# Filler matmuls on TensorE behind the last unit of the slot iterations and in the last normalisation

## The chip, the cores and the metric

One core of one Trainium2 chip runs the whole kernel as one launch. The metric is the device time in microseconds; the profile shows one execution of the same program.

## The reference

The computation is two layers on 16 batches of 56 tokens with 128 features, beside a context of 16 x 1500 x 128. What matters here is the second half:

```python
x = x + cross_attention_0(layernorm(x), ctx)      # 16 heads
x = x + ffn_0(layernorm(x))                       # fake-quantised, 384 wide
x = x + slot_attention(layernorm(x), ctx)         # 3 iterations, below
x = x + experts(layernorm(x))                     # 8 experts, 512 wide, summed

def slot_attention(slots, P):
    k, v = project(rmsnorm(P))
    for _ in range(3):
        q = rmsnorm(slots) @ Wq.T
        attn = softmax(q @ k.T * scale, axis=-2)  # over the 56 slots
        attn = attn / (sum(attn, axis=-1) + 1e-6)
        updates = attn @ v
        slots = gru_cell(updates, slots)
    return slots
```

The layer norm in front of the experts is the last normalisation: mean, centring, variance, square root, reciprocal, product.

## The kernel before

Tokens lie along the free dimension: `xT`, `stream` and the like are [128 features, 896 tokens]. PSUM is one tensor `ps` of eight banks of 512 fp32 columns; the banks 4 to 7 have names in the slot iterations: UPD (4), TURN (5), GATES (6), QUERY (7).

Each engine has a program of its own, written out by hand; an instruction starts when the one ahead of it on its engine lets it and when the semaphores waited for have come. There is no scheduler behind it.

**Slot iterations.** 3 iterations x 16 batches are 48 units of four slots each. In a unit TensorE makes the scores of one batch (L1590, 36 matmuls), VectorE finds the maxima and sums, ScalarE the exponentials (L784), GpSimd weighs them (L583). Four units are a quad; there are `GROUPS_C` = 12 quads, 4 per iteration. Each quad is followed by a string of stages, which `iterations` places some slots after the quad's begin, beside the units of later quads:

- `update_sums(0)` and `update_sums(1)` (offsets 19 and 27): the attend matmuls of two units each, L1606, into UPD
- `update_rows` on VectorE (L1203 to L1209): division by the sums
- `turn_updates` (offset 35): two transposes, L1616; ScalarE copies them out (L793)
- `gate_sums` (offset 39): six products in fp32 of `stream` and the copied updates, two passes each, L1624 to L1627
- ScalarE's tanh (L800, L806) and VectorE's GRU steps (L1218 to L1229), which write the new slots into `stream`
- `slot_means` (offset 51) and what follows from it up to the next queries, in bank QUERY: only for the quads 0 to 7, since the last iteration has no next queries.

For the last quad (11) the later stages come after the last unit's scores, in this order on TensorE: gates of quad 10, attend matmuls of the second pair of quad 11, its transposes, its gates. There is nothing else to do then.

**Last normalisation.** VectorE adds `stream` to `xT` (L1271, `x3_done`). `layernorm(3)` on TensorE makes the means (L1303, two fp32 products of 448 columns), waits for ScalarE's squares of what VectorE centred (L845, L635), makes the variance (L1308), waits for square root (ScalarE L640) and reciprocal (VectorE L849), and spreads the result over the rows (L1314). VectorE multiplies (L855) and splits the result in two fp16 halves (L1277, L1279). In VectorE's own queue, the first expert's weights are split on the way: `weights_high(0)` (L1263) behind the centring, `weights_low(0)` (L1267) behind the reciprocal. `layernorm` of TensorE takes two hooks, `after_means` and `after_variance`, which the fourth normalisation leaves empty.

**Experts.** 64 units (8 experts x 4 blocks x 2 halves of the tokens), nine fp16 products of 448 columns each (L1646 to L1648), whose results go through ScalarE (L823, L828), VectorE (L1285) and GpSimd (L619).

The kernel has a filler of the same sort elsewhere, `keep_busy`, in the feed-forward stage and in the third normalisation, whose lines are L1551 (means), L1554 (variance), L1512 (eight fillers) and L1559 (spread):

```python
def keep_busy(n):
    for _ in range(n):
        nc.tensor.matmul(ps[:, 5, 0:512], ctx_hi[:, 0, 0:128], ctx_hi[:, 0, 0:512], start=True, stop=True)
```

Of the kernel before, what the change touches and what calls it, by code (L numbers as in the profile page):

```python
# [65 lines left out]
def wait(engine, semaphore, value):  # L66

    if isinstance(value, int) and value <= 0:
        return
    engine.wait_ge(semaphore, value)  # L70
# [21 lines left out]
def build(nc, dram, out):  # L92
    with ExitStack() as ctx:
        def sbuf(name, shape, dt=F32, stack=ctx):
            return stack.enter_context(nc.sbuf_tensor(name, shape, dt))
# [4 lines left out]
        ps = ctx.enter_context(nc.psum_tensor("ps", [128, 8, 512], F32))  # L100
# [100 lines left out]
        query_hi = sbuf("query_hi", [128, T], F16, stack=sc)  # L201
# [38 lines left out]
        GROUPS_C = UNITS_C // QUAD  # L240
# [68 lines left out]
        UPD, TURN, GATES, QUERY = 4, 5, 6, 7  # L309
# [27 lines left out]
        def quad(g):  # L337
            return bass.ts(g % PER_IT, QT)
# [9 lines left out]
        def rows_of(n):  # L348

            return n % BATCH if n % BATCH < RESIDENT else RESIDENT + streamed_load(n) % STREAMED  # L350

        def rows_landed(n):

            return 16 if n % BATCH < RESIDENT else 16 * (streamed_load(n) // STREAMED + 1)
# [267 lines left out]
        def _(act):  # L622
# [7 lines left out]
            def layernorm_sd(n, after_squares=None):  # L630
                _, centred, squared, _ = NORMS[n]
                wide = WIDE[n]
                for h in range(2):
                    act.wait_ge(ln_centred, 2 * n + h + 1)
                    nc.scalar.activation(squared[:, bass.ts(h, wide)], centred[:, bass.ts(h, wide)], ACT.Square).then_inc(ln_squared, 1)  # L635
                if after_squares:
                    after_squares()
                act.wait_ge(ln_var, n + 1)
                wait(act, ln_rstd, n)
                nc.scalar.activation(sd[:, 0:wide // 2], ps[:, 2, 0:wide // 2], ACT.Sqrt, bias=eps_ln[:]).then_inc(ln_sd, 1)  # L640
# [121 lines left out]

            load_table(ACT.Sqrt)
            _, centred, squared, _ = NORMS[2]
            for h in range(2):
                act.wait_ge(ln_centred, 4 + h + 1)
# [70 lines left out]
        def _(dve):  # L837
            def layernorm(n, after_squares=None, after_roots=None):

                src, centred, _, dst = NORMS[n]  # L840
                wide = WIDE[n]
                for h in range(2):
                    at = bass.ts(h, wide)
                    dve.wait_ge(ln_mean, 2 * n + h + 1)
                    nc.vector.tensor_tensor(centred[:, at], src[:, at], ps[:, h, 0:wide], ALU.subtract).then_inc(ln_centred, 1)  # L845
                if after_squares:
                    after_squares()
                dve.wait_ge(ln_sd, n + 1)
                nc.vector.reciprocal(rstd[:, 0:wide // 2], sd[:, 0:wide // 2]).then_inc(ln_rstd, 1)  # L849
                if after_roots:  # L850
                    after_roots()
                for h in range(2):
                    at = bass.ts(h, wide)
                    dve.wait_ge(ln_spread, 2 * n + h + 1)
                    nc.vector.tensor_tensor(dst[:, at], centred[:, at], ps[:, SPREAD[n][h], 0:wide], ALU.mult).then_inc(ln_out, 1)  # L855
# [442 lines left out]
        def _(pe):  # L1298
            def layernorm(n, after_means=None, after_variance=None):
                src, _, squared, _ = NORMS[n]  # L1300
                wide = WIDE[n]
                for i in range(2):
                    nc.tensor.matmul(ps[:, i, 0:wide], ones_mean[:], src[:, bass.ts(i, wide)], start=True, stop=True).then_inc(ln_mean, 1)  # L1303
                if after_means:
                    after_means()
                pe.wait_ge(ln_squared, 2 * (n + 1))
                for i in range(4):
                    last = nc.tensor.matmul(ps[32 * i:32 * i + 32, 2, 0:wide // 2], ones_mean[:, 0:32], squared[:, bass.ts(i, wide // 2)], start=True, stop=True)  # L1308
                last.then_inc(ln_var, 1)
                if after_variance:  # L1310
                    after_variance()
                pe.wait_ge(ln_rstd, n + 1)
                for i in range(4):
                    last = nc.tensor.matmul(ps[:, SPREAD[n][i // 2], bass.ts(i % 2, wide // 2)], spread[:, i, :], rstd[:, 0:wide // 2], start=True, stop=True)  # L1314
                    if i % 2:
                        last.then_inc(ln_spread, 1)
# [213 lines left out]
            for i in range(4 * F0):  # L1530
                if i == 9:
# [4 lines left out]
                                 start=True, stop=True).then_inc(f_ready, 1)  # L1536
# [12 lines left out]
            _, _, squared, _ = NORMS[2]  # L1549
# [18 lines left out]
            def late_spread():  # L1568

                pe.wait_ge(ln_rstd, 3)  # L1570
                for i in range(4):
                    last = nc.tensor.matmul(ps[:, LATE_SPREAD + i // 2, bass.ts(i % 2, GW)], spread[:, i, :], rstd[:], start=True, stop=True)
                    if i % 2:
                        last.then_inc(ln_spread, 1)

            def unit(n, k):
# [14 lines left out]
                if k == SLOTS - 1:  # L1591
                    last.then_inc(c_scores, 1)
                    if n == 1:
                        late_spread()

            def update_sums(pair):
                def sums(g):
                    m = 2 * g + pair
                    pe.wait_ge(c_attended, 2 * m + 2)
                    for n in (2 * m, 2 * m + 1):  # L1600
                        pe.wait_ge(rows_loaded[rows_of(n)], rows_landed(n))
                    wait(pe, u_rows_done, g)
                    for c in range(NCH):
                        for j in range(2):
                            n = 2 * m + j
                            last = nc.tensor.matmul(ps[64 * j:64 * j + TOK, UPD, (D + 1) * pair:(D + 1) * (pair + 1)], c_prob[n % PROBS][:, c, :],  # L1606
                                                    ctx_rows[:, rows_of(n), c, :],
                                                    start=(c == 0), stop=(c == NCH - 1), skip_group_check=True)
                    last.then_inc(u_ready, 1)
                return sums  # L1610

            def turn_updates(g):
                pe.wait_ge(u_rows_done, g + 1)
                wait(pe, tanh_done, g)
                for i in range(2):
                    last = nc.tensor.transpose(ps[:, TURN, bass.ts(i, D)], u_rows[:, i, :], ident32[:])  # L1616
                last.then_inc(u_turned, 1)

            def gate_sums(g):
                slots = stream[:, quad(g)]  # L1620
                pe.wait_ge(u_copied, g + 1)
                wait(pe, slots_done, g)
                for i in range(2):
                    nc.tensor.matmul(ps[:, TURN, bass.ts(i, QT)], whhT[:, bass.ts(i, D)], slots, start=True, stop=False)  # L1624
                    nc.tensor.matmul(ps[:, TURN, bass.ts(i, QT)], to_gates[:, bass.ts(i, D)], updT, start=False, stop=True)
                nc.tensor.matmul(ps[:, GATES, QT:2 * QT], whhT[:, 2 * D:3 * D], slots, start=True, stop=True)
                nc.tensor.matmul(ps[:, GATES, 0:QT], to_gates[:, 2 * D:3 * D], updT, start=True, stop=True).then_inc(gates_ready, 1)  # L1627

            def slot_means(g):
# [4 lines left out]

            iterations(unit, [
                (TENSOR_AT["means"], True, slot_means), (TENSOR_AT["turn"], False, turn_updates), (TENSOR_AT["gates"], False, gate_sums),
                (TENSOR_AT["sums"][0], False, update_sums(0)), (TENSOR_AT["sums"][1], False, update_sums(1))])


            pe.wait_ge(x3_done, 1)  # L1640
            layernorm(3)

            def product(bank, w, w_at, x_high, x_low, first, last):

# [92 lines left out]
```

## Time and profile before

| | |
|---|---|
| median of the runs | 814.04 us |
| lowest and highest of 3 | 813.88, 817.6 us |
| the profiled execution | 809.81 us |
| its span, first to last instruction | 808.0 us |
| mean granted TensorE clock | 0.925 |
| TensorE busy | 683.6 us, 85% |
| VectorE, ScalarE, GpSimd busy | 581.7, 533.2, 435.5 us |

Busy time is a share of the whole span; the stages differ. The granted clock is the share of 2.4 GHz that TensorE was given; it has two levels here, 1.0 and 0.5, and a figure between them is a mean over a stretch that has both. A matmul's record holds the time in which its result drains, so neighbouring records overlap.

### The profile page before, as it was taken

To read this page: it belongs to the slowest core of one execution; us is meant where nothing else is said; L and a number is where in the kernel's file an instruction comes from. 1 tells how busy PE (TensorE), PEld (TensorE's weight loads), DVE (VectorE), ACT (ScalarE), POOL (GpSimd) and SP (SyncE) were. 2 spreads that over 40 slices of the span, in tenths; PEclk is the share of its full clock that TensorE was granted. 3 is DMA by queue.
4 is the path that set the end of the run, shared out by engine and by line. 5 is a ranking of instruction groups with operands and counts; after the bars stand their busy time and mean duration, and the time that the engine had idled before them with its cause. 6 is when DMAs were issued, how large, how long until landed. Compare 5 with 4: busy or idle time off the path is not lost.

```text
span 808.0 us, 23757 instructions
## 1 busy us (share of the span) xinstructions
PE 683.6 (85%) x8878; PEld 492.1 (61%) x8878; DVE 581.7 (72%) x1073; ACT 533.2 (66%) x1158; POOL 435.5 (54%) x476
## 2 busy tenths in 40 slices
PE   5789599999999999997835678888788875899997
PEld 2267377777777777775522468887778863444443
DVE  5878387878878787887786667778777755665663
ACT  3266276777777776765462699899988962555554
POOL 1647847777777777742000044666666520566664
PEclk9799699999999999999876979999888995999999
DMA  5532634444444444330500504532540540112100
GB/s 192 138 109 74 178 97 136 133 132 132 128 134 129 131 126 133 92 88 14 188 0 3 234 2 160 196 123 93 218 166 2 181 136 26 53 41 79 39 2 24
DMA packets 26720, 86.15 MB, mean 107 GB/s; under 512 B 5829, under 2 KB 7493, under 8 KB 26645
## 3 DMA queue, kind: packets, MB, share of 16 engines
q1 hardware_dynamic: 26264, 84.73, 33.1%
q8 instruction: 46, 0.75, 0.4%
q10 hardware_dynamic: 384, 0.46, 0.2%
q14 instruction: 26, 0.21, 0.1%
HBM read 65.19 MB, written 0.46 MB: 81 GB/s over the span
## 4 chain that ended last, share of the span: by engine, by line
PE 45%; DVE 17%; POOL 14%; ACT 9%; issue 8%; SPq 4%; DMA 2%; POOLq 0%; DVEq 0%; ACTq 0%
POOL ctx_lo L619 9%; PE ps L1350 8%; PE ps L1367 7%; PE ps L1381 6%; ACT c_prob L784 4%; PE ps L1337 4%; PE ps L1606 3%; SPq L436 3%; PE ps L1590 3%; PE ps L1326 3%; DVE tile_max L870 2%; PE ps L1386 2%; DVE ps L1171 2%; ACT w0T L784 2%; DVE amax_part L1086 1%
## 5 line engine op out<-in xcount | busy, mean ns | idle before, releaser
L870 DVE TENSOR_REDUCE tile_max<-ps 128x1 f32<-128x500 f32 x336 | 215.0, 675 | 51.4 <-PE ps L1350 51.0
L645 ACT ACTIVATE probs<-ps 125x896 f32<-125x896 f32 x192 | 175.3, 916 | 95.9 <-PE ps L1367 95.0
L1350 PE MATMUL ps<-k_hi,qdiag 128*128 128x500 f16 x336 | 130.4, 390 | 6.9 <-DVE tile_max L870 2.8
L784 ACT ACTIVATE c_prob<-ps,c_bias,row_scale 125x56 f32<-125x56 f32 x384 | 116.0, 473 | 6.9 <-DVE c_bias L1174 6.9
L619 POOL TENSOR_TENSOR ctx_lo<-ctx_hi,ctx_lo 128x448 f16<-128x448 f32 x64 | 72.1, 1127 | 70.7 <-ACT ctx_lo L828 70.7
L1367 PE MATMUL ps<-qstack,kstack 98*125 98x224 f16 x768 | 107.1, 263 | 0.4
L583 POOL TENSOR_TENSOR c_prob<-c_prob,c_weight 125x672 f32<-125x672 f32 x32 | 42.0, 1311 | 115.6 <-DVE c_weight L1188 115.5
L1367 PEld LDWEIGHTS ps<-qstack,kstack 98*125 98x125 f16 x768 | 86.7, 137 | 21.1 <-ACT probs L645 2.8
L1590 PE MATMUL ps<-query_hi,ctx_hi 128*128 128x56 f16 x576 | 55.9, 195 | 34.1 <-ACT c_prob L784 24.7
L1381 PE MATMUL ps<-probs,v_aug 125*32 125x168 f32 x1536 | 75.4, 314 | 3.3 <-ACT probs L645 2.5
L1590 PEld LDWEIGHTS ps<-query_hi,ctx_hi 128*128 128x128 f16 x576 | 49.6, 101 | 40.5 <-ACT c_prob L784 23.8
L1646 PE MATMUL ps<-ctx_lo 128*128 128x448 f16 x192 | 67.8, 353 | 6.9 <-DVE ctx_hi L1285 3.2
L538 POOL TENSOR_TENSOR rows_in<-rows_in 125x768 f32<-125x768 f32 (+2 forms) x96 | 68.8, 717 | 7.5
L1285 DVE SCALAR_TENSOR_TENSOR ctx_hi<-ctx_hi,ps 128x448 f32<-128x448 f32 x64 | 38.8, 616 | 45.4 <-ACT ctx_hi L823 45.4
L823 ACT ACTIVATE ctx_hi<-ps 128x448 f32<-128x448 f32 x64 | 34.8, 543 | 51.7 <-PE ps L1648 51.5
L523 POOL TENSOR_TENSOR qstack<-q_rep,slot_mask 96x224 f16<-96x224 f32 (+1 forms) x64 | 33.7, 556 | 63.2 <-PE ps L1367 58.1
L1648 PE MATMUL ps<-ctx_lo 128*128 128x448 f16 x192 | 67.7, 352 | 0.0
L1647 PE MATMUL ps<-ctx_lo 128*128 128x448 f16 x192 | 67.7, 352 | 0.0
L1171 DVE TENSOR_REDUCE ps<-ps 125x12 f32<-125x672 f32 x48 | 41.3, 860 | 26.9 <-PE ps L1590 26.9
L1381 PEld LDWEIGHTS ps<-probs,v_aug 125*32 125x32 f32 x1536 | 40.4, 109 | 32.3 <-issue 24.4
L1590 PE MATMUL ps<-query_hi,ctx_lo 128*128 128x56 f16 x576 | 55.8, 194 | 0.0
L1590 PE MATMUL ps<-query_lo,ctx_hi 128*128 128x56 f16 x576 | 55.6, 194 | 0.0
(262 smaller groups left out, 1702.4 us busy)
## 6 DMA issues: line engine op xcount, KB each, us to landing
row_tiles<-in_ctx_rows_wide SPq DMA_DIRECT2D x40, 774.0 KB, 5.7
ctx<-in_ctxT SPq DMA_DIRECT2D x16, 750.0 KB, 5.4
rows_in<-in_ctx_rows SPq DMA_DIRECT2D x16, 750.0 KB
kstack<-k_hi SPq DMA_DIRECT2D x128, 93.8 KB, 2.8
kstack<-k_lo SPq DMA_DIRECT2D x64, 93.8 KB, 2.7
ctx_hi<-in_wg SPq DMA_DIRECT2D x8, 256.0 KB, 2.7
ctx_hi<-in_wu SPq DMA_DIRECT2D x8, 256.0 KB, 3.0
ctx_hi<-in_wd SPq DMA_DIRECT2D x8, 256.0 KB, 3.5
```

Source lines behind the costliest of these rows:

```text
L538: nc.gpsimd.tensor_tensor(a, a, z, ALU.add).then_inc(rows_step, 1)
L619: nc.gpsimd.tensor_tensor(hidden_lo[i], hidden[i], hidden_hi[i], ALU.subtract).then_inc(h_lo_done, 1)
L645: nc.scalar.activation(probs[c % RING_P][0:CH, :].rearrange("p (k w) -> p k w", k=2), score_tile(c)[0:CH], ACT.Exp, scale=float(HD) ** -0. ...
L784: last = nc.scalar.activation(c_prob[n % PROBS][:, c, :], ps[0:CH, 2 * (n % 2) + c // 6, bass.ts(c % 6, TOK)], ACT.Exp, bias=c_bias[n % 2] ...
L870: nc.vector.reduce_max(tile_max[:, u % MAXT, u // MAXT:u // MAXT + 1], ps[:, MAXB + (u + p) % 2, 0:KCOLS], AX.X).then_inc(max_done, 1)
L1350: nc.tensor.matmul(ps[:, MAXB + (u + p) % 2, 0:KCOLS], qdiag[p][:, bass.ts(t, 128)], k_hi[p][:, bass.ts(j, KCOLS)], start=True, stop=True) ...
L1367: last = nc.tensor.matmul(ps[0:CH, 2 * (c % 2) + g // 2, bass.ts(g % 2, GW)], kstack[p][0:STACK_ROWS, g, bass.ts(c, CH)], qstack[p][0:STAC ...
L1381: nc.tensor.matmul(ps[GR * g:GR * g + GR, OUTB, 0:three], v_aug[p][0:CH, of, g, HD:], probs[of % RING_P][0:CH, GW * g:GW * g + three], sta ...
L1590: last = nc.tensor.matmul(ps[:, 2 * (n % 2) + c // 6, bass.ts(c % 6, TOK)], l, r, start=(j == 0), stop=(j == 2))
L1646: nc.tensor.matmul(bank, w1_hi[w][:, at], x_high, start=first, stop=False)
L1647: nc.tensor.matmul(bank, w1_lo[w][:, at], x_high, start=False, stop=False)
L1648: return nc.tensor.matmul(bank, w1_hi[w][:, at], x_low, start=False, stop=last)
```

## The change

A function `keep_warm(g, n)` issues n matmuls of [128x128] by [128x512] in fp16 into bank QUERY, for the last quad alone. It is called with 4 ahead of the second pair's attend matmuls, 4 ahead of the transposes and 3 ahead of the gates, each time before the waits of that stage; then with 18 ahead of the wait for `x3_done`, 5 behind the means, 7 behind the variance, and 9 behind the spread: 50 in all.

```diff
+            def keep_warm(g, n):
+
+                if g == GROUPS_C - 1:
+                    for _ in range(n):
+                        nc.tensor.matmul(ps[:, QUERY, 0:512], query_hi[:, 0:128], query_hi[:, 0:512], start=True, stop=True)
+
             def update_sums(pair):
                 def sums(g):
+                    keep_warm(g, 4 * pair)
                     m = 2 * g + pair
                     pe.wait_ge(c_attended, 2 * m + 2)
...
             def turn_updates(g):
+                keep_warm(g, 4)
                 pe.wait_ge(u_rows_done, g + 1)
...
             def gate_sums(g):
                 slots = stream[:, quad(g)]
+                keep_warm(g, 3)
                 pe.wait_ge(u_copied, g + 1)
...
+            last_quad = GROUPS_C - 1
+            keep_warm(last_quad, 18)
             pe.wait_ge(x3_done, 1)
-            layernorm(3)
+            layernorm(3, after_means=lambda: keep_warm(last_quad, 5), after_variance=lambda: keep_warm(last_quad, 7))
+            keep_warm(last_quad, 9)
```

## Rows read from the trace of the kernel before

**Rows 1.** The page, part 2: granted clock in 40 equal slices, in tenths.

```profile
PEclk9799699999999999999876979999888995999999
```

**Rows 2.** Stretches: their length, busy time of each engine (instructions), clock, DMA.

```profile
core 0: us, PE busy (x) PEld busy (x) DVE busy (x) ACT busy (x) POOL busy (x), PEclk, DMA share, GB/s
437.30:460.00 22.70, 16.61 (x144) 9.64 (x145) 11.98 (x18) 11.88 (x28) 0.00 (x0) 1.00 0.53 210
656.70:659.40 2.70, 2.54 (x12) 2.19 (x12) 1.29 (x4) 0.95 (x5) 0.90 (x3) 1.00 0.54 204
663.10:665.40 2.30, 0.62 (x6) 0.20 (x2) 1.82 (x6) 0.34 (x1) 0.00 (x0) 1.00 0.00 0
...
665.90:669.30 3.40, 3.40 (x11) 2.98 (x9) 0.00 (x0) 0.00 (x0) 0.00 (x0) 0.51 0.00 0
669.40:672.80 3.40, 0.23 (x2) 0.00 (x0) 2.08 (x6) 2.17 (x4) 0.00 (x0) 0.99 0.00 0
672.90:686.30 13.40, 7.68 (x20) 3.87 (x20) 7.59 (x9) 3.54 (x7) 0.00 (x0) 0.50 0.08 26
686.50:690.00 3.50, 1.62 (x9) 0.89 (x10) 1.76 (x3) 0.27 (x1) 0.00 (x0) 1.00 0.29 107
...
692.00:796.00 104.00, 101.00 (x528) 50.82 (x527) 64.36 (x74) 59.70 (x118) 66.91 (x60) 1.00 0.12 39
```

**Rows 3.** The chain that ended last, in order of time: start, length, what.

```profile
669.03 0.61 PE ps L1627 x2
...
674.72 3.37 PE ps L1303 x4
...
682.52 3.37 PE ps L1314 x8
...
685.91 0.63 DVE stream L855
```

**Rows 4.** TensorE in order of time; in brackets its idle time before, and the releaser.

```profile
660.41 0.32 PE L1606 MATMUL ps<-row_tiles,merge_w 125*56 125x129 f32 x1 [1.08 <-POOL w0T L583]
...
664.20 0.44 PE L1616 MATMUL ps<-ident,u_rows 128*128 128x128 f32 x2 [0.92 <-DVE u_rows L1209]
665.44 0.62 PE L1624 MATMUL ps<-stream,whhT 128*128 128x224 f32 x2 [0.80 <-DVE stream L1229]
...
674.72 3.35 PE L1303 MATMUL ps<-xT,ones_mean 128*128 128x448 f32 x4 [5.09 <-DVE xT L1271]
679.40 0.97 PE L1308 MATMUL ps<-work,ones_mean 128*32 128x224 f32 x8 [1.32 <-ACT work L635]
682.52 3.35 PE L1314 MATMUL ps<-rstd,spread 128*128 128x224 f32 x8 [2.15 <-DVE rstd L849]
688.38 0.36 PE L1646 MATMUL ps<-ctx_lo 128*128 128x448 f16 x1 [2.50 <-DVE ctx_lo L1279]
```

**Rows 5.** The same view of TensorE around the third normalisation.

```profile
434.68 2.34 PE L1512 MATMUL ps<-ctx_hi 128*128 128x512 f16 x5
...
443.21 1.77 PE L1551 MATMUL ps<-xT,ones_mean 128*128 128x448 f32 x4 [0.78 <-DVE xT L1133]
446.30 0.59 PE L1554 MATMUL ps<-work,ones_mean 128*32 128x224 f32 x8 [1.32 <-ACT work L767]
446.82 1.90 PE L1512 MATMUL ps<-ctx_hi 128*128 128x512 f16 x8
449.04 1.78 PE L1559 MATMUL ps<-work,spread 128*128 128x224 f32 x8 [0.32 <-DVE work L1142]
```

**Rows 6.** VectorE and ScalarE in order of time, in both normalisations.

```profile
447.44 1.55 DVE L1142 RECIPROCAL work<-work 128x224 f32<-128x224 f32 x1 [1.79 <-ACT work L769]
...
450.32 1.17 DVE L1149 TENSOR_TENSOR work<-work,ps 128x448 f32<-128x448 f32 x2
...
664.67 0.34 ACT L793 COPY work<-ps 128x224 f32<-128x224 f32 x1 [3.14 <-PE ps L1616]
...
680.92 1.55 DVE L849 RECIPROCAL rstd<-sd 128x224 f32<-128x224 f32 x1 [1.31 <-ACT sd L640]
682.39 1.70 DVE L1267 SCALAR_TENSOR_TENSOR ctx_lo<-ctx_hi,ctx_lo 128x1536 f16<-128x1536 f32 x1
```

## The prediction

> **What bounds the kernel now.** I read the slices of the page first, for the granted clock. The row of clocks [rows 1] is at 8 or 9 tenths over most of the span, and its lowest digit, a 5, stands in the seventh-last place, which at 20.2 us a slice is 667 to 687 us. That is where most of the added matmuls go. So the second view is a table of stretches around that place [rows 2]. The reader is to see three things in its clock column: TensorE holds its upper level (1.00, 2.4 GHz) until about 665.9 us; from there to 669.3 us it works with no idle at 0.51, the lower level (1.2 GHz); and after an interval at 0.99, in which it did next to nothing, it is at 0.50 again from 672.9 to 686.3 us. From 686.5 us it is at 1.00 to the end.
>
> Third, the chain of waits, to see whether the slow stretches set the end. They do: the chain [rows 3] goes through the last gate products, which begin at 665.44 us [rows 4] and end at 669.64 us, the four mean matmuls (3.37 us) and the spread (3.37 us), with the variance (0.97 us, [rows 4]) and steps of VectorE and ScalarE between them. Nothing runs beside these: all the units are finished, and every engine waits for this one string. The gates belong to the last quad; they are released by VectorE's L1229, the new slots of the quad before, and need the copy of this quad's updates as well.
>
> Behind it lies the expert stage, 119.6 us from 688.38 us on. There TensorE is busy 101.00 of 104 us at full clock [rows 2], so that stage has a length of its own, and whatever is won ahead of it moves its start and the end of the kernel alike. Its weights wait on nothing here: the first two experts' loads are issued when the last scores are done.
>
> **What the change adds.** Nothing is removed or moved. It adds 50 matmuls of 128x512 in fp16 (4, 4, 3, 18, 5, 7, 9 in program order), each with its weight load, all into bank 7, which nobody reads or writes in this part: its users, the slot means and projected queries, exist only for the first eight quads, and the copy of query_hi that the fills read is written no more. No fill signals anything and none waits; but what is queued behind a fill on TensorE waits for it. No DMA, and no work for another engine, is added.
>
> The price of one fill at the upper level: the expert stage did 528 matmuls of 448 columns in 101.00 us, 0.191 us each, so 512 columns are an estimated 0.219 us [rows 2]. The old kernel has the same kind of filler: eight of them took 1.90 us, 0.24 us each with the last one's drain [rows 5]. At the lower level five took 2.34 us; I take 0.44 us each, twice the first figure.
>
> Now each group of fills against the idle time of TensorE that it stands in [rows 4]:
> 4 fills, 0.88 us, ahead of L1606 (the last 48 attend matmuls): idle 1.08 us.
> 4 fills, 0.88 us, ahead of the transposes L1616: idle 0.92 us. This is the tight one, but the copy L793 that hangs on the transposes is done at 665.01 us [rows 6], 0.43 us before the gates start, so a small overrun is still covered.
> 3 fills, 0.66 us, ahead of the gates L1624: idle 0.80 us.
> 18 fills, 3.94 us, ahead of the means L1303: idle 5.09 us. Queued behind them are the means, and for those wait VectorE's centring and everything after.
> 5 fills, 1.10 us, ahead of the variance L1308: idle 1.32 us.
> 7 fills, 1.53 us, ahead of the spread L1314: idle 2.15 us.
> 9 fills, 1.97 us, ahead of the first expert product L1646: idle 2.50 us, and more once the spread is fast.
> All are covered at the upper level, so I cost them at nothing. If that cover is gone, that is, at the lower level, they overrun by 0.7, 0.8, 0.5, 2.8, 0.9, 0.9 and 1.5 us; 6.1 us for the last four, all on the chain.
>
> Could the fills slow VectorE or ScalarE through PSUM or SBUF? The reciprocal L1142 that ran beside eight fillers took 1.55 us, and L849, the same shape with TensorE idle, took 1.55 us [rows 6]. So zero, and the other bound is the rounding of these two rows.
>
> **What the clock gives back.** If the fills keep the clock up, four pieces shrink; each has a twin at the upper level in this same trace.
> Gates: 665.44 to 669.64 us is 4.20 us; the same twelve matmuls of the quad before were busy 2.54 us [rows 2 to 4]. Saves 1.66 us.
> Means: 3.35 us against 1.77 us for L1551, same shape, same count [rows 4, 5]. Saves 1.58 us.
> Variance: 0.97 against 0.59 us for L1554. Saves 0.38 us.
> Spread: 3.35 against 1.78 us for L1559. Here not all of the 1.57 us is won, because VectorE is late next: in its queue L1267 (weights_low of the first expert) stands between the reciprocal and L855 and ends at 684.09 us, 1.57 us after the spread starts [rows 6]. Today L855 waits for TensorE; then it waits for L1267. From there two of them take about 1.17 us (L1149, same shape, two in a row) and 0.02 us of start, so the pair ends 2.76 us after the spread's start, against 4.02 us now (685.91 + 0.63 - 682.52) [rows 3]. Saves 1.26 us.
> The sum is 1.66 + 1.58 + 0.38 + 1.26 = 4.88 us.
>
> The profiled execution took 809.81 us for a span of 808.0 us, so the sum gives 804.9 us for it. The median of the runs shown is 814.04 us, 4.2 us more than that execution and 0.16 us from the lowest. I take the same saving from the median: 814.04 - 4.88 = 809.2 us, which is 0.6% less.
>
> **Will the clock stay up?** The best row is the third normalisation. It is the same string of work, with eight fillers behind its variance, and over 437.3 to 460 us the clock was 1.00 throughout, though TensorE was busy for only 16.61 of 22.70 us [rows 2]; it idled 1.32 us ahead of L1554 and 0.32 us ahead of L1559 [rows 5]. With the fills, the stretch of the change has idle times of about 0.2 to 1.2 us between much longer work: 3.9 us of fills where nothing ran now. The fall at 665.9 us came after a stretch in which TensorE was busy for 0.62 of 2.30 us [rows 2]; 7 fills bring that to about 2.2 us. The fall at 672.8 us came after 0.23 us of work in 3.40 us; there the 18 fills stand.
>
> The Trainium skill ("TensorE: Matmul & The Clock Gate", "Why this matters for your kernels") blames a loss of clock on long idle gaps between bursts of matmuls. By that rule the short gaps of 0.92 and 0.80 us would not be what lowers the clock over the gates, filling them would buy nothing there, and the sum would be 3.2 us. The trace doesn't agree: the clock did fall after just those gaps. A second rule of the same page ("A second HAM failure mode: psum-queue depth-cycling") speaks against the change: frequent micro-idles between groups of matmuls let the clock swing between its levels, and the fills leave such idles. The third normalisation has them too and kept 1.00.
>
> **Rivals.**
> *The gates gain nothing.* Either the clock falls over them all the same, or, in the executions that are timed, it had not fallen there before. For it: that fall was late, in the middle of a busy engine, and its place must depend on more than this stretch; the profiled execution was 4.2 us off the median, so its falls needn't be those of the others. Against it: the fills make the stretch before the gates dense. Saving 4.88 - 1.66 = 3.22 us: 806.6 us for the profiled execution, 810.8 us at the median, 0.4% less.
> *More than the sum.* In the profiled execution the clock was back at 686.4 us, 2 us ahead of the expert stage. Where it comes back later, the first twelve expert matmuls run at half pace, 12 x 0.191 = 2.3 us, and the fills would win that too: 7.2 us, 806.8 us at the median.
> *The change doesn't do what it says.* The fills are issued, are covered, and the clock falls anyway for the means and the spread, because short work with gaps isn't enough once the string goes through VectorE. Then time stays at 814.0 us. Against it stands the third normalisation.
> *Slower.* The clock is at its lower level when the 18 fills begin and stays there. It decides from the point where a fill costs more than 5.09/18 = 0.28 us; at 0.44 us the last four groups overrun by 6.1 us and give nothing back: 820.1 us at the median. For it: five fillers at 434.68 us did run at the lower level. Against it: behind those five the clock was up again before 437.3 us, so a run of 18 would lift it before it ends.
>
> **How the numbers follow.** What a measurement of this kernel can tell from no change is about 0.5%, here 4.1 us. Chances: the sum as worked out 0.46; gates gain nothing 0.26; more than the sum 0.12; no effect 0.09; slower 0.07. The predicted time is that of the likeliest, 809.2 us. Faster by over 0.5% are the first and the third, less the part of the first that falls short of 4.1 us and with the part of the second that reaches it: 0.57. Within 0.5%: 0.36. Slower: 0.07. The range reaches from somewhat below the larger saving (806.8, less the 2 us by which medians of so few runs may shift when single ones lie between 809.8 and 817.6) to just short of no effect: 804.8 to 813.4 us.
>
> **What would show it.** Right: gates L1624 to L1627 busy about 2.5 us, L1303 1.8, L1308 0.6, L1314 1.8 us; the clock 1.00 from the last units into the expert stage; L855 starting right behind L1267; means still starting on VectorE's x3 and not on a fill; the expert stage as long as before. Wrong: a granted clock of 0.5 under any of these lines, a fill as the last thing ahead of L1303, L1308, L1314 or L1646, or the whole gain present in this part while the iterations ahead of it, which the change doesn't touch, run differently and hide it.

## The result

| | median us | lowest to highest | runs |
|---|---|---|---|
| before | 813.96 | 812.3 to 817.6 | 6 |
| changed | 805.51 | 803.83 to 807.81 | 6 |

The changed kernel takes 0.9894 of the old time (95% interval 0.9865 to 0.9922), which is 8.45 us less at the median. The forecast was 4.88 us less, 809.2 us, with a range of 804.8 to 813.4 us. The direction, the range and the mechanism held; the size at the median is 1.7 times the sum. Two later measurements of the same pair gave 5.3 and 6.85 us. Most of what follows is about that surplus.

The profiled execution of the changed kernel took 803.83 us for a span of 802.0 us, 6.0 us less than the old one's span. First its granted clock by slices, which answers to [rows 1]:

```profile
PEclk9799899999999999999976979899988899999999
```

The 5 in the seventh-last place is gone; the dips further left are those of the slot iterations and the earlier stages. Next a table of stretches, to be read against [rows 2] (columns as there):

```profile
662.20:664.50 2.30, 2.17 (x13) 0.79 (x10) 1.82 (x6) 0.35 (x1) 0.00 (x0) 1.00 0.00 0
664.50:667.10 2.60, 2.58 (x14) 2.39 (x15) 0.00 (x0) 0.04 (x1) 0.00 (x0) 1.00 0.00 0
667.10:672.10 5.00, 3.81 (x18) 1.55 (x16) 3.49 (x7) 2.68 (x5) 0.00 (x0) 1.00 0.01 2
672.10:682.40 10.30, 8.78 (x41) 4.24 (x41) 8.05 (x9) 3.09 (x5) 0.00 (x0) 1.00 0.18 55
641.80:798.60 156.80, 146.95 (x954) 80.64 (x950) 93.46 (x132) 85.18 (x186) 78.36 (x73) 1.00 0.15 51
```

The clock is 1.00 in every one of them; the last row says that it didn't fall once from 641.8 us to 798.6 us. The first row is the stretch ahead of the gates: TensorE was busy 0.62 of 2.30 us before, and 2.17 of 2.30 us now. Then TensorE in order of time, which answers to [rows 4]; L1600 are the fills, L1613 the old L1606, L1633 the old L1624, L1658 the old L1646:

```profile
658.23 1.03 PE L1600 MATMUL ps<-query_hi 128*128 128x512 f16 x4
659.49 0.32 PE L1613 MATMUL ps<-row_tiles,merge_w 125*56 125x129 f32 x1 [0.23 <-POOL w0T L583]
...
662.29 1.04 PE L1600 MATMUL ps<-query_hi 128*128 128x512 f16 x4
663.28 0.44 PE L1624 MATMUL ps<-ident,u_rows 128*128 128x128 f32 x2
663.55 0.81 PE L1600 MATMUL ps<-query_hi 128*128 128x512 f16 x3
664.51 0.62 PE L1633 MATMUL ps<-stream,whhT 128*128 128x224 f32 x2
...
666.86 4.05 PE L1600 MATMUL ps<-query_hi 128*128 128x512 f16 x18
672.12 1.77 PE L1303 MATMUL ps<-xT,ones_mean 128*128 128x448 f32 x4 [1.21 <-DVE xT L1271]
673.73 1.24 PE L1600 MATMUL ps<-query_hi 128*128 128x512 f16 x5
675.21 0.58 PE L1308 MATMUL ps<-work,ones_mean 128*32 128x224 f32 x8 [0.24 <-ACT work L635]
675.73 1.69 PE L1600 MATMUL ps<-query_hi 128*128 128x512 f16 x7
677.95 1.78 PE L1314 MATMUL ps<-rstd,spread 128*128 128x224 f32 x8 [0.54 <-DVE rstd L849]
679.57 2.11 PE L1600 MATMUL ps<-query_hi 128*128 128x512 f16 x9
682.41 0.36 PE L1658 MATMUL ps<-ctx_lo 128*128 128x448 f16 x1 [0.73 <-DVE ctx_lo L1279]
```

The reader is to see that ahead of L1303, L1308, L1314 and L1658 some idle time is left, and that each is released by VectorE or ScalarE, not by a fill: the cover holds. The transposes (L1624) and the gates (L1633) stand right behind fills with no idle time shown. They are not late for it: they start 3.79 and 5.02 us after the L1613 in the second row, and started 3.79 and 5.03 us after the same L1606 before. The means take 1.77 us instead of 3.35, the variance 0.58 instead of 0.97, the spread 1.78 instead of 3.35. VectorE behind the spread answers to the late-next step of the forecast:

```profile
677.81 1.69 DVE L1267 SCALAR_TENSOR_TENSOR ctx_lo<-ctx_hi,ctx_lo 128x1536 f16<-128x1536 f32 x1
679.42 1.14 DVE L855 TENSOR_TENSOR stream<-work,ps 128x448 f32<-128x448 f32 x2
```

L855 has no idle time before it any more: it waits for L1267 in its own queue, as forecast.

From here on, "the stretch" is the time from the first attend matmul (L1606) of the last quad's second pair (660.41 us before) to the first expert product (688.38 us). The recorded expectations call this the first L1606 behind the last scores; strictly, the first pair's attend matmuls (from 652.95 us) and the transposes of quad 10 come behind the last scores too. It took 27.97 us before and takes 22.92 us now (682.41 - 659.49). That is 5.05 us, where the sum said 4.88. The expert stage, from there to the end of the span, took 119.62 and takes 119.62 us. (Spans are taken to a hundredth of a us here; the expectations have some of these sums from spans rounded to a tenth, up to 0.05 us away.) The remaining 0.92 us between the two spans (660.41 against 659.49) lies ahead of the stretch, in code that the change doesn't touch.

### The profile page after: what moved, and what is told of

It reads as the page before. It is cut to its first block, busy times and chain, and to the rows that moved or that the text cites. A ratio compares the mean times of both kernels' runs of the same rounds, so it can differ in the third digit from the quotient of the medians.

```text
span 802.0 us, 23857 instructions
## 1 busy us (share of the span) xinstructions
PE 689.1 (86%) x8928; PEld 493.5 (62%) x8928; DVE 579.7 (72%) x1073; ACT 533.7 (67%) x1158; POOL 436.4 (54%) x476
## 4 chain that ended last, share of the span: by engine, by line
PE 43%; DVE 19%; POOL 16%; issue 8%; ACT 6%; SPq 4%; DMA 2%; POOLq 0%; DVEq 0%; ACTq 0%
POOL ctx_lo L619 9%; PE ps L1350 8%; PE ps L1367 7%; PE ps L1381 6%; PE ps L1337 4%; PE ps L1613 3%; ACT c_prob L784 3%; SPq L436 3%; PE ps L1326 3%; DVE tile_max L870 2%; PE ps L1590 2%; DVE ps L1171 2%; PE ps L1386 2%; DVE c_sum L1182 1%; DVE amax_part L1086 1%
## 5 line engine op out<-in xcount | busy, mean ns | idle before, releaser
L1658 PE MATMUL ps<-ctx_lo 128*128 128x448 f16 x192 | 67.8, 353 | 5.1 <-DVE ctx_hi L1285 3.2
```

What stands on the lines that cost most here:

```text
L1658: nc.tensor.matmul(bank, w1_hi[w][:, at], x_high, start=first, stop=False)
```

## The experiments

### One part at a time

`e1_before_again` is the old kernel, unchanged.

> The old kernel, unchanged, profiled once more and timed against itself: ratio 1.000 within 0.4%. In the two profiles at hand the stretch from the first L1606 behind the last scores to the first expert product took 27.97 us before and 22.92 us after, 5.05 us less, while the medians differ by 8.45 us. Theory 'the rest is in the stretch': another execution of the old kernel has its low clock elsewhere and a stretch (with the first expert units) of 29 to 32 us, 2 to 4 us more than the first profile had. Theory 'the rest is ahead of it': the stretch is again within 0.5 us of 28.0 us, and the executions differ in the slot iterations (454 to 657 us in the first profile) by several us.

Measured: 1.0001 of before (0.9979 to 1.0022). In its profile the stretch took 25.90 us (664.86 to 690.76) and the expert stage 121.07 us, together 146.97 us against 147.59 us in the first profile. The low clock lay in other places. Stretches of this execution:

```profile
674.60:681.30 6.70, 3.35 (x4) 1.17 (x4) 3.30 (x6) 2.08 (x4) 0.00 (x0) 0.50 0.00 1
681.50:684.70 3.20, 0.59 (x8) 0.16 (x8) 2.27 (x2) 2.43 (x4) 0.00 (x0) 1.00 0.00 0
684.90:688.10 3.20, 3.19 (x8) 2.53 (x8) 2.18 (x2) 0.00 (x0) 0.00 (x0) 0.50 0.13 39
...
691.70:694.90 3.20, 3.20 (x10) 1.26 (x9) 0.62 (x1) 0.76 (x2) 0.00 (x0) 0.50 0.00 0
```

and its TensorE at the last gate products and the means:

```profile
671.85 0.54 PE L1627 MATMUL ps<-work,to_gates 128*128 128x224 f32 x2
677.49 3.35 PE L1303 MATMUL ps<-xT,ones_mean 128*128 128x448 f32 x4 [5.09 <-DVE xT L1271]
```

Here the gates ran at full clock (0.54 us for a pair, as in their twins), and the price was paid elsewhere: the first expert units, from 691.7 to 694.9 us, ran at half the clock. So neither theory as I put it holds: the stretch was shorter, not longer, and 1.4 us of loss had moved into the expert stage. Half of the second theory is there: from the first scores to the stretch this execution took 209.50 us, the first one 206.95 us.

`e2_gates_only` keeps the fills around the last quad's updates alone:

```diff
-            keep_warm(last_quad, 18)
+            keep_warm(last_quad, 0)
...
-            layernorm(3, after_means=lambda: keep_warm(last_quad, 5), after_variance=lambda: keep_warm(last_quad, 7))
-            keep_warm(last_quad, 9)
+            layernorm(3, after_means=lambda: keep_warm(last_quad, 0), after_variance=lambda: keep_warm(last_quad, 0))
+            keep_warm(last_quad, 0)
```

> Only the 11 fills around the last quad's updates (4, 4, 3), none in the normalisation. Theory of the sum: gates 2.5 us instead of 4.2, nothing else, so 1.7 us (0.2%) faster than before. Rival 'the gates gain nothing': in timed executions the clock has mostly not fallen there, 0 to 0.5 us. Rival 'more than the sum': the part that the prediction missed is here or is in the return of the clock ahead of the experts, which these fills don't touch.

Measured: 811.28 us, 0.998 of before (0.9963 to 0.9997), by that ratio 1.6 us less. This is near the 1.7 us of the sum, but the interval reaches from 0.2 to 3.0 us and so holds the rival's upper end as well. Its profile shows that not every execution gains: stretch 25.92 and expert stage 121.08 us, together 147.00 us, as much as the old kernel's 146.97 us in `e1`, where the gates ran at full clock without any fills. The low clock came later:

```profile
673.60:680.20 6.60, 3.36 (x4) 1.18 (x4) 3.25 (x6) 2.03 (x3) 0.00 (x0) 0.50 0.00 1
...
690.60:693.80 3.20, 3.20 (x11) 1.23 (x9) 0.62 (x1) 0.70 (x2) 0.00 (x0) 0.50 0.03 5
```

`e3_norm_only` keeps the other 39:

```diff
-                    keep_warm(g, 4 * pair)
+                    keep_warm(g, 0 * pair)
...
-                keep_warm(g, 4)
+                keep_warm(g, 0)
...
-                keep_warm(g, 3)
+                keep_warm(g, 0)
```

> Only the 39 fills behind the last gates (18, 5, 7, 9), none ahead of the gates. Theory of the sum: means, variance and spread at full clock, 3.3 us (0.4%) faster than before, the gates at 4.2 us if the low clock falls on them. Rival 'the gates gain nothing': as fast as the whole change, about 8 us less than before. If the missing 3.5 us come from a late return of the clock, they are here too: 6 to 8 us.

Measured: 807.86 us, 0.9948 of before (0.9912 to 0.9983), 4.2 us less by the ratio, between the 3.3 us of the sum and the 6 to 8 us of a late return; its interval (1.4 to 7.1 us) holds the 3.3 as well as the 6, but not the 8 us of "the gates gain nothing". The stretch took 24.11 us, the expert stage 119.62 us. In its profile the clock fell over the gates, as in the old kernel's first profile but later in them:

```profile
670.54 0.62 PE L1633 MATMUL ps<-stream,whhT 128*128 128x224 f32 x2
670.96 0.95 PE L1634 MATMUL ps<-work,to_gates 128*128 128x224 f32 x2
...
673.20 4.59 PE L1600 MATMUL ps<-query_hi 128*128 128x512 f16 x18
678.50 1.77 PE L1303 MATMUL ps<-xT,ones_mean 128*128 128x448 f32 x4 [0.71 <-DVE xT L1271]
```

The 18 fills behind them began at the low clock (4.59 us instead of 4.05), were still over 0.71 us before the means were due, and the means ran fast. The missing 11 fills cost this execution 1.19 us, 24.11 against 22.92. It also answers the rival "slower": 18 fills began at the low clock, it came back while they ran, and they stayed covered.

`e4_after_again` and `e9_after_third` are the changed kernel, unchanged.

> The whole change once more, on the same chip as the three beside it: 0.989 of before, within 0.3%. The stretch at 22.9 us again; what differs between its executions is ahead of it, in the slot iterations.

Measured: 807.03 us, 0.9932 of before (0.9902 to 0.9962), against a median of 812.35 us before. That misses the 0.989 within 0.3% that I expected, though the two intervals overlap. Stretch 22.92, expert stage 119.62 us.

> The whole change once more, to settle its size. Stretch and expert stage saved 4.4 to 5.1 us in the profiles; the two measurements of the medians gave 8.45 and 5.3 us. Theory 'the surplus is chance ahead of the stretch': 4.5 to 6.5 us less than before (0.992 to 0.9945), stretch 22.9 us. Rival 'the old kernel is often worse in the stretch than the profiles showed': 7 us or more again (0.991 or lower).

Measured: 806.82 us, 0.9915 of before (0.9883 to 0.9947), before 813.67 us. Stretch 22.92, expert stage 119.62 us. The ratio lies between the two theories and its interval holds both, so it doesn't decide between them.

### The old kernel's own spread

> The old kernel once more, for its profile alone. So far the old kernel's stretch (first L1606 behind the last scores to first expert product) and its expert stage together took 147.59 and 146.94 us, the changed kernel's 142.51 and 142.52 us. Theory 'what the fills save depends on where the falls land': this third one is between 146 and 151 us, with low clock in at least two separate intervals behind 665 us, over the gates or over the first expert products. Rival 'the rest lies ahead': again 147 us.

Measured in its profile: stretch 27.98, expert stage 119.61, together 147.59 us, with the clock low from 668.6 to 672.0 us (over the gates) and from 675.4 to 689.1 us. That is the pattern of the first profile again. It has the two intervals of the theory and nearly the 147 us of the rival, so it does not decide between them.

> The old kernel, for its profile alone: stretch and expert stage together 146.9 to 147.7 us, as in the three profiles so far (theory), or 149 us and more in an execution with its low clock placed worse (rival).

Measured: stretch 27.51 and expert stage 121.85, together 149.36 us. The rival was right for this execution. Its stretches and a part of its TensorE:

```profile
666.80:688.00 21.20, 10.15 (x27) 5.58 (x25) 11.74 (x16) 5.81 (x10) 0.00 (x0) 0.50 0.11 37
688.00:693.90 5.90, 5.87 (x16) 2.40 (x17) 1.22 (x3) 1.54 (x3) 0.10 (x1) 0.50 0.00 0
694.10:704.00 9.90, 9.53 (x51) 4.55 (x49) 7.09 (x8) 5.94 (x12) 6.73 (x6) 1.00 0.14 49
```

```profile
688.03 0.56 PE L1646 MATMUL ps<-ctx_lo 128*128 128x448 f16 x1 [2.50 <-DVE ctx_lo L1279]
689.12 0.58 PE L1646 MATMUL ps<-ctx_lo 128*128 128x448 f16 x1
...
694.37 0.35 PE L1646 MATMUL ps<-ctx_lo 128*128 128x448 f16 x1
```

The clock fell over the gates and was back only at 694 us, 6 us into the expert stage. The L1646 matmuls, every third of the stream, start 1.1 us apart before that and take 0.58 us; behind it they take 0.35 us.

### How much cover there is

`e6_doubled` doubles the last four groups of fills:

```diff
-            keep_warm(last_quad, 18)
+            keep_warm(last_quad, 36)
...
-            layernorm(3, after_means=lambda: keep_warm(last_quad, 5), after_variance=lambda: keep_warm(last_quad, 7))
-            keep_warm(last_quad, 9)
+            layernorm(3, after_means=lambda: keep_warm(last_quad, 10), after_variance=lambda: keep_warm(last_quad, 14))
+            keep_warm(last_quad, 18)
```

> As the whole change, but 36, 10, 14 and 18 fills instead of 18, 5, 7 and 9. Theory of the sum (a fill is worth 0.219 us at full clock and is covered only while it fits): the means start 2.8 us late, the variance 0.9, the spread 0.9 and the experts 1.1 us late, in all 5.7 us more than the change, so about the time of the old kernel (0.998 to 1.005). If fills were dropped or overtaken at a wait, the time would be that of the change.

Measured: 812.67 us, 1.0004 of before (0.998 to 1.0028): the whole gain is spent. Its stretch took 27.85 us, 4.93 us more than the change's 22.92, where I expected 5.7. TensorE in order of time:

```profile
667.95 7.93 PE L1600 MATMUL ps<-query_hi 128*128 128x512 f16 x36
675.72 1.67 PE L1303 MATMUL ps<-xT,ones_mean 128*128 128x448 f32 x4
677.22 2.32 PE L1600 MATMUL ps<-query_hi 128*128 128x512 f16 x10
679.47 0.58 PE L1308 MATMUL ps<-work,ones_mean 128*32 128x224 f32 x8
679.99 3.20 PE L1600 MATMUL ps<-query_hi 128*128 128x512 f16 x14
683.02 1.68 PE L1314 MATMUL ps<-rstd,spread 128*128 128x224 f32 x8
```

No brackets: the work that matters starts behind the last fill. 36 fills less one drain of 0.38 us are 35 steps of 0.216 us, the price of one. The estimate was 0.219 us, and the fills also begin before the record of the work ahead of them has ended, which I hadn't counted: together some 0.2 us for each group. The same can be read from the change: 39 more fills are 8.4 us of work, and the stretch grew by 4.93 us, so 3.5 us of them were still covered, where the brackets of the changed kernel show 2.72 us of idle time (1.21 + 0.24 + 0.54 + 0.73).

`e7_eighteen_only` takes the 5, 7 and 9 away and keeps the rest:

```diff
-            layernorm(3, after_means=lambda: keep_warm(last_quad, 5), after_variance=lambda: keep_warm(last_quad, 7))
-            keep_warm(last_quad, 9)
+            layernorm(3, after_means=lambda: keep_warm(last_quad, 0), after_variance=lambda: keep_warm(last_quad, 0))
+            keep_warm(last_quad, 0)
```

> The 4, 4, 3 and 18 fills, without the 5, 7 and 9 inside the normalisation. Theory 'one dense run carries the clock through, as in the third normalisation': as the whole change within 0.5 us. Rival 'the gaps inside must be filled too': TensorE then works 1.8, 0.6 and 1.8 us with gaps of 1.3, 2.1 and 2.9 us, the clock falls during the spread or over the first expert products, in some executions, and 1 to 3 us are given back.

Measured: 808.75 us, 0.9961 of before (0.9939 to 0.9982), 3.4 us less at the median, where the whole change gained 5.3 to 8.45. The intervals of the ratios overlap those of `e4` and `e9`, so the times alone do not settle it, but the profile does for its execution, and there the rival was right. A stretch of its profile, and its spread:

```profile
681.60:688.30 6.70, 4.20 (x12) 1.46 (x11) 3.54 (x6) 0.54 (x1) 0.00 (x0) 0.50 0.39 120
```

```profile
680.14 2.04 PE L1314 MATMUL ps<-rstd,spread 128*128 128x224 f32 x8 [2.15 <-DVE rstd L849]
684.67 0.55 PE L1658 MATMUL ps<-ctx_lo 128*128 128x448 f16 x1 [2.50 <-DVE ctx_lo L1279]
```

The clock held for the means and the variance, fell in the middle of the spread and came back at 688.4 us. Stretch 23.00, expert stage 121.42 us: 1.9 us lost against the whole change, nearly all of it in the first expert units. So in this execution the small groups were missed by the experts, not by the normalisation.

### The same idea in the slot iterations

The dips left in the clock behind the first 25 us of the iterations are one for each quad, behind an idle time of some 2.5 us ahead of every fourth unit. `e8_iter_fill` adds to the change:

```diff
                 if k == 0:
+                    if n >= 8 and n % QUAD == 0:
+                        pe.wait_ge(u_rows_done, n // QUAD - 1)
+                        for _ in range(16):
+                            nc.tensor.matmul(ps[:, UPD, 258:512], ctx_hi_flat[:, 0:128], ctx_hi_flat[:, 0:254], start=True, stop=True)
                     wait(pe, c_exped, n - 1)
```

> The whole change, and 16 fills of 254 columns into unused columns of bank UPD ahead of every fourth unit of the slot iterations from unit 8 on, where TensorE idles about 2.5 us and the clock falls for 3.4 us right behind (ten times). It adds a wait on u_rows_done that the transposes four slots later have anyway. Theory 'the clock is what makes TensorE late at the quad's begin': cold L1632, L1633, L1616 and L1606 cost up to 1.7 us a quad, 5 to 15 us less than the change (0.6 to 1.8%). Rival 'ScalarE, busy 184 of 203 us there, sets the pace': under 2 us less. Against both, fills of 1.75 us that meet a shorter gap would push the scores back.

Measured: 803.94 us, 0.989 of before (0.9857 to 0.9923). From the first scores to the first L1606 of the stretch it took 206.20 us, against 208.81, 209.28 and 209.32 us in the three profiles of the change. The group of its fills (busy us, mean ns, idle before, releaser):

```profile
L1585 PE MATMUL ps<-ctx_hi 128*128 128x254 f16 x160 | 22.5, 303 | 19.5 <-DVE u_rows L1209 19.5
```

TensorE stood idle 19.5 us for the fills' own wait, and the clock still fell at 512.5, 567.1 and 601.2 us. Most of that idle time is not new: from 475 to 655 us the changed kernel idles 27.4 us ahead of its scores, this one 1.0 us there and 19.5 us ahead of the fills. `e10_turn_fill` fills in a bank that is long free at that point:

```diff
                 if k == 0:
+                    if n >= 8 and n % QUAD == 0:
+                        wait(pe, tanh_done, n // QUAD - 2)
+                        for _ in range(9):
+                            nc.tensor.matmul(ps[:, TURN, 0:512], ctx_hi_flat[:, 0:128], ctx_hi_flat[:, 0:512], start=True, stop=True)
                     wait(pe, c_exped, n - 1)
```

> The whole change, and ahead of every fourth unit from unit 8 on nine fills of 512 columns into bank TURN instead of the sixteen shorter ones into UPD. The wait that guards them, on tanh_done, is long over there, while the wait on u_rows_done of the kernel before it made TensorE idle 19.5 us in ten places. Theory 'that wait ate part of the gain': no falls of the clock between 475 and 657 us and 1 to 6 us less than the kernel with fills in UPD, 0.982 to 0.988 of before. Rival 'ScalarE sets the pace': 0.989 again. A fall of the clock in the iterations would mean that nine fills don't suffice.

Measured: 802.26 us, 0.9865 of before (0.9829 to 0.9901), against 0.9915 for the change, measured beside it. It is the fastest kernel here. Its fills show no idle time before them, the iterations from first scores to stretch take 203.81 us, and the clock over most of them is 0.99; from 475 us on one fall, at 517.1 us, is left, so the expectation of none was missed. The group of fills, then the iterations as a stretch:

```profile
L1585 PE MATMUL ps<-ctx_hi 128*128 128x512 f16 x90 | 21.0, 378 | 0.0
```

```profile
475.00:655.00 180.00, 161.00 (x2857) 138.49 (x2852) 138.85 (x348) 167.14 (x566) 107.51 (x159) 0.99 0.40 141
```

The same stretch of the changed kernel:

```profile
475.00:655.00 180.00, 151.76 (x2658) 140.58 (x2658) 135.58 (x341) 162.96 (x551) 105.68 (x155) 0.89 0.39 140
```

Its 5.0 to 5.5 us less in the iterations come with a clock of 0.99 instead of 0.89. ScalarE is busy 167 of 180 us now, so both theories seem to have a part: the clock made TensorE late, and with 0.99 little is left to win from it. That ScalarE sets the pace from here on was not tested. Against `e8` it is 2.4 us less in the iterations, within the 1 to 6 us expected for the needless wait; but `e10` also has two falls of the clock fewer and other fills, so the price of the wait alone is not shown.

## Why the prediction was right, and where its size was off

**The fills are covered.** Right, with 0.23 to 1.21 us to spare where the rows show idle time, and with the transposes and the gates on time where they show none. The doubled kernel shows the other side: past its cover the string waits for the fills, at 0.216 us each.

**The clock stays up.** Right: 1.00 without a break from 641.8 to 798.6 us, and all three profiles of the change have a stretch of 22.92 us. Over the gates the clock fell in three of the four profiles of the old kernel and in `e3`, which has no fills there (3.70 to 4.19 us for the twelve matmuls, 2.51 us in `e1`); in all eight profiles with the 11 fills it did not fall, and the gates took 2.51 us each time. Two rules of the Trainium skill ("TensorE: Matmul & The Clock Gate") had been weighed. By "Why this matters for your kernels" filling the short gaps would gain the gates nothing; the trace disagrees, they gained where the clock had fallen on them. By "A second HAM failure mode: psum-queue depth-cycling" the idles left would let the clock swing; with idle times of 0.23 to 1.21 us it didn't, while without the small groups, at 1.32, 2.15 and 2.50 us, it fell (`e7`), which is what that rule describes.

**The four terms.** Gates 665.44 to 669.64 us, now 664.51 to 667.02: 1.69 us (forecast 1.66). Means 3.35 to 1.77: 1.58 (1.58). Variance 0.97 to 0.58: 0.39 (0.38). The spread and the two L855 behind it: 4.02 us before, now from 677.95 to 680.56, 2.61 us: 1.41 (1.26); the two L855 took 1.14 us in a row and followed L1267 without a gap. For the profiled pair the sum was right within 0.2 us.

**The step that was mis-sized** is the one from the profiled execution to the median: "I take the same saving from the median". The old kernel does not lose the same in each execution. Its stretch and expert stage together took 147.59, 146.97, 147.59 and 149.36 us in four profiles, the changed kernel's 142.54 us in all three. So the fills save 4.4 to 6.8 us, 5.3 us on average, and what varies is where the clock falls and when it returns. The two rivals that I had kept apart are both there, and one compensates the other: in `e1` the gates gain nothing, but 1.4 us of the expert stage is won (121.07 against 119.62); in `e11` the gates gain 1.2 us and 2.2 us of the expert stage comes on top, 6.8 us in all where "more than the sum" said 7.2. The term at fault is the one I set at zero for the likeliest case, the expert units at low clock; it measured 0.0, 1.4, 0.0 and 2.2 us. It is worth 0.9 us on average, not the whole surplus. The first measurement, 805.51 us, stands only 0.7 us above the lower end of the range, and since part of the surplus has no explanation, that it fell inside is in part luck.

**What stays open.** The three measurements of the change gave 8.45, 5.3 and 6.85 us between medians (ratios 0.9894, 0.9932, 0.9915, whose intervals overlap). Their mean is 6.9 us, and the profiles of stretch and expert stage account for 5.3. The other 1.6 us are not explained. The profiles show where such a surplus can sit. The changed kernel's three spans are on average 6.3 us shorter than the old one's four: 5.3 us shorter in stretch and expert stage, 1.9 us shorter ahead of the first scores (452.1 against 454.0 us), and 0.9 us longer in the iterations. Ahead of the first scores the code is the same in both. The iterations go with the clock: they took 206.95 and 206.94 us in the two old profiles in which the clock was low for 47.8 us of them, and 208.8 to 209.6 us in the other two and in the three of the change, with 51.2 us at the low clock. Executions of the same old kernel reached the start of the stretch anywhere from 660.41 to 664.86 us, and those of the changed kernel from 659.49 to 662.41 us, with the same instructions up to there but for four fills; chance in that part is large enough for it, but that it is chance was not shown.

## What to carry to other kernels

Where one string of short steps on several engines sets the end, look at TensorE's granted clock along it: if its matmuls run at the low level, filler matmuls into a bank that nobody uses can double their speed, provided that each group fits the idle time it stands in. Let the fills wait for nothing late; what such a wait costs was not measured by itself. Price the fill from the doubled case (here 0.216 us for 512 columns) and stop short of the gap; doubling the last four groups gave the whole gain back. Don't take what the clock costs from one profile: profile the old kernel several times, since the falls can land elsewhere the next time, and what they miss in one stage they may hit in the next.

## What the runs showed that was not expected

The low clock is not tied to a place in the program. In four executions of the same kernel it began behind the last units at 665.9, 674.5, 668.6 and 666.7 us, and was back for good at 686.4, 695.0, 689.1 and 694.0 us. And a single dense run of fills (18, 3.9 us) does not carry the clock through what follows: in `e7` it fell 8 us after the last of them, in the middle of a busy spread, although idle times of no more than 2.15 us lay between.
